# A fused audio-tower kernel: VectorE adds the embedding's bias on the way out of PSUM, gamma and beta move to the passes after it

## The reference

```python
# tokenizer: patches of 16 rows of x, stride 8, 124 tokens per batch element
y  = einsum('bpi,di->bpd', patches, W) + b                 # D = 256
h  = (y - mean(y)) * rsqrt(var(y) + EPS) * gamma + beta
# attention layer on the normalised h
n  = layernorm(h); q, k, v = n@Wq.T+bq, n@Wk.T+bk, n@Wv.T+bv
h  = h + softmax(q @ k.T / scale) @ v
# mixture of experts: 6 experts, the best 2 for each token
n  = layernorm(h)
p  = softmax(relu(n @ router_w1 + b1) @ router_w2 + b2); top_w, top_i = top_k(p, 2)
e  = relu(relu(n @ w1 + b1) @ w2 + b2) @ w3 + b3           # per expert
h  = h + sum(e[top_i] * softmax(top_w))
```

## Time and profile before

| what | value |
|---|---|
| three runs | 1249.2, 1250.46, 1252.42 us (median 1250.46) |
| profiled execution | 1249.82 us, of which the span from the first to the last instruction is 1248.0 us |
| PE busy | 1197.6 us, 96% of the span, 7792 instructions |
| DVE busy | 984.9 us, 79% |
| ACT busy | 893.4 us, 72% |
| POOL busy | 901.1 us, 72% |
| first half | up to about 600 us; PE idle 0.2 us between 300 and 480 us |

### The profile page before, as it was taken

The page is one execution under the profiler, slowest core; times in us unless marked ns, Lnnn a source line. Parts: engine busy times, 40 slices in busy tenths (PEclk is TensorE's granted clock), DMA queues, the critical chain, the costliest instruction groups (busy, mean ns, idle before and its releaser), DMA issues. The chain is left out here.

```text
span 1248.0 us, 27869 instructions
## 1 busy us (share of the span) xinstructions
PE 1197.6 (96%) x7792; PEld 1060.7 (85%) x7792; DVE 984.9 (79%) x3213; ACT 893.4 (72%) x2093; POOL 901.1 (72%) x684
## 2 busy tenths in 40 slices
PE   6999999999999999999789999999999999999993
PEld 5888988889888988887678888889888888888883
DVE  5678888888888988886796887778778777787773
ACT  4788888888888888887456667666676666766762
POOL 2227888888888888887788676767667667676776
PEclk9999999999999999999899999999999999999997
DMA  4334665554454545564589988776886797697655
GB/s 132 111 94 121 164 166 148 143 128 131 128 128 123 129 130 142 169 168 117 139 189 279 238 155 206 119 128 108 174 180 113 130 225 126 116 203 150 111 60 60
DMA packets 137190, 180.43 MB, mean 145 GB/s; under 512 B 38344, under 2 KB 103500, under 8 KB 137036
## 3 DMA queue, kind: packets, MB, share of 16 engines
q0 software_dynamic: 75456, 69.19, 34.5%
q1 hardware_dynamic: 60316, 108.67, 28.6%
q10 hardware_dynamic: 1264, 0.79, 0.2%
HBM read 159.01 MB, written 101.49 MB: 209 GB/s over the span
## 5 line engine op out<-in xcount | busy, mean ns | idle before, releaser
L570 POOL DMA_INDIRECT out<-yo,tail x268 | 432.5, 1614 | 169.1 <-issue 139.6
L522 POOL DMA_INDIRECT expert_rows<-rec,row_i x256 | 356.3, 1392 | 78.0 <-issue 67.2
L1003 ACT ACTIVATE h2v<-bank,small 128x512 f32<-128x512 f32 x134 | 92.3, 690 | 205.3 <-PE bank L793 189.8
L820 PE MATMUL bank<-w_sb,h_hi 128*128 128x256 f32 x1072 | 208.7, 288 | 3.5 <-issue 3.4
L793 PE MATMUL bank<-x_hi,w_sb 128*128 128x512 f32 x536 | 178.2, 394 | 6.1 <-DVE x_lo L1380 4.6
L793 PE MATMUL bank<-h_hi,w_sb 128*128 128x512 f32 x536 | 177.2, 391 | 1.8 <-issue 1.8
L820 PEld LDWEIGHTS bank<-w_sb,h_hi 128*128 128x128 f32 x1072 | 171.3, 191 | 4.4 <-issue 4.3
L820 PE MATMUL bank<-w_sb,h_lo 128*128 128x256 f32 x536 | 151.5, 283 | 0.0
L793 PEld LDWEIGHTS bank<-x_hi,w_sb 128*128 128x128 f32 x536 | 101.7, 190 | 27.9 <-issue 4.8
L793 PEld LDWEIGHTS bank<-h_hi,w_sb 128*128 128x128 f32 x536 | 100.9, 188 | 21.9 <-issue 1.9
L1009 ACT ACTIVATE yo<-yo,gcol 128x256 f32<-128x256 f32 x268 | 113.9, 498 | 4.5 <-DVE yo L1411 4.5
(11 more groups left out here) (193 smaller groups left out, 2975.9 us busy)
## 6 DMA issues: line engine op xcount, KB each, us to landing
w_sb<-split_weights SPq DMA_DIRECT2D x189, 512.0 KB
xg<-expert_rows SPq DMA_DIRECT2D x67, 530.0 KB
out<-h SPq DMA_DIRECT2D x32, 496.0 KB
split_weights<-half_w SPq DMA_DIRECT2D x36, 256.0 KB
small<-in_esmall SPq DMA_DIRECT2D x67, 134.0 KB
x_in<-in_x SPq DMA_DIRECT2D x32, 250.0 KB
expert_rows<-pad_rows SPq DMA_DIRECT2D x9, 530.0 KB
raw_w<-in_eweights SPq DMA_DIRECT2D x36, 128.0 KB
```

The costliest lines, as they stand in the source:

```text
L522: pool.indirect_dma_start(rows_dram, bass.IndirectOffsetOnAxis(ap=row_i[0:TOK, slot, j, k:k + 1], axis=0), rec[0:TOK, slot, j, :], None).t ...
L570: pool.indirect_dma_start(out, bass.IndirectOffsetOnAxis(ap=tail[:, t % TAILS, j, E8:].bitcast(I32), axis=0), yo[:, t % YO, j, :], None, c ...
L820: mm = pe.matmul(banks[6 + b][:, (j % 2) * D:(j % 2 + 1) * D], act[:, c, j * P:(j + 1) * P], w[:, 2, c, wh, :], start=(c == 0 and p == 0), ...
L1003: act.activation(h2v[:, m, :], banks[bank + m][:], ACT.Relu, bias=small[:, t % SLOTS, DC + m:DC + m + 1]).then_inc(S["h2_v"], 1)
```

## The change

The bias is loaded once into all 128 partitions (`bias_bc`) and centred there; the bias matmul and its operands go. VectorE's pass out of PSUM adds the bias instead of multiplying by gamma, and stands right behind the statistics of h instead of behind those of the attention. Gamma becomes the last factor of the h pass, and beta is added by two new instructions over h. ScalarE squares y out of SBUF, behind `pT` instead of ahead of `qT`. `shifts` (the column `nmr`) moves ahead of the split of x. `LN1_N` becomes 17.

```diff
-LN1_N, AV_N, TOPK_N, POS_N = 15, 14, 23, 4
+LN1_N, AV_N, TOPK_N, POS_N = 17, 14, 23, 4
...
-            sp.wait_ge(S["pool_const"], 1)
-            for r in (0, 32):
-                sp.dma_start(bias_raw["tok"][r:r + 1, :], tok_b).then_inc(S["tok_bias_loaded"], 16)
+            sp.dma_start(bias_bc[:], tok_b.to_broadcast([P, D])).then_inc(S["tok_bias_loaded"], 16)
...
                             for c in range(DC):
-                                product(into, [t[:, at + c:at + c + TOK] for t in (xT_hi, xT_lo)],
-                                        [proj["tok"][:, b, c, :] for b in range(2)], c == 0, False)
-                            if it == -1:
-                                pe.wait_ge(S["proj_low"], 2)
-                            mm = pe.matmul(into, ones_r[:, 0:TOK], bias_row["tok"][:], start=False, stop=True)
+                                mm = product(into, [t[:, at + c:at + c + TOK] for t in (xT_hi, xT_lo)],
+                                             [proj["tok"][:, b, c, :] for b in range(2)], c == 0, c == DC - 1)
...
-                if xa:
-                    g, slot, rnd = xa
-                    wait(act, S["rstd13"], deviations(g - 2))
-                    for j in range(GB):
-                        act.wait_ge(S["tok_ps"], g * 2 + j // 2 + 1)
-                        wait(act, S["squares"], g * GB + j)
-                        act.activation(square[0:TOK, :], banks[6 + j // 2][0:TOK, (j % 2) * D:(j % 2 + 1) * D], ACT.Square,
-                                       scale=D ** -0.5, accum_out=mv[0:TOK, 0, j, 1:2]).then_inc(S["squares"], 1)
                 if x1:
...
                     act.activation(pT[0:TOK + 1, :], banks[4][0:TOK + 1, 0:GT], ACT.Identity).then_inc(S["pT_sb"], 1)
+                if xa:
+                    g, slot, rnd = xa
+                    wait(act, S["rstd13"], deviations(g - 2))
+                    for j in range(GB):
+                        act.wait_ge(S["ln1"], g * LN1_N + 1 + j // 2)
+                        wait(act, S["squares"], g * GB + j)
+                        act.activation(square[0:TOK, :], y[0:TOK, j, :], ACT.Square,
+                                       scale=D ** -0.5, accum_out=mv[0:TOK, 0, j, 1:2]).then_inc(S["squares"], 1)
                 if x3:
...
+                    if it == 0:
+                        v.wait_ge(S["const_loaded"], N_CONST)
                     for j in range(GB):
                         v.wait_ge(S["ln1"], at + 1 + j // 2)
                         v.scalar_tensor_tensor(out=h[R, g % KEPT, j, :], in0=y[R, j, :], scalar=rstd[R, 0, j:j + 1],
-                                               in1=beta_bc[R, :], op0=ALU.mult, op1=ALU.add).then_inc(S["ln1"], 1)
+                                               in1=gamma_bc[R, :], op0=ALU.mult, op1=ALU.mult).then_inc(S["ln1"], 1)
+                    for pair in range(2):
+                        v.wait_ge(S["ln1"], at + 4 + 2 * pair)
+                        v.tensor_tensor(h[R, g % KEPT, 2 * pair:2 * pair + 2, :], h[R, g % KEPT, 2 * pair:2 * pair + 2, :],
+                                        beta_bc[R, :].unsqueeze(1).to_broadcast([TOK, 2, D]), ALU.add).then_inc(S["ln1"], 1)
...
                 if it == 0:
                     fold_weights()
                     shifts(0)
+                if xa:
+                    g, slot, rnd = xa
+                    for pair in range(2):
+                        v.wait_ge(S["tok_ps"], g * 2 + pair + 1)
+                        v.tensor_tensor(y[R, 2 * pair:2 * pair + 2, :],
+                                        banks[6 + pair][R, :].rearrange("p (b n) -> p b n", b=2),
+                                        bias_bc[R, :].unsqueeze(1).to_broadcast([TOK, 2, D]), ALU.add
+                                        ).then_inc(S["ln1"], 1)
                 if x4:
                     gates(*x4)
...
-
+                if x0 and it > 0:
+                    shifts(x0[0])
                 if xs:
...
-                if x0 and it > 0:
-                    shifts(x0[0])
                 if it == DRAIN - 2:
...
-                    for pair in range(2):
-                        v.wait_ge(S["squares"], g * GB + 2 * pair + 2)
-                        v.tensor_tensor(y[R, 2 * pair:2 * pair + 2, :],
-                                        banks[6 + pair][R, :].rearrange("p (b n) -> p b n", b=2),
-                                        gamma_bc[R, :].unsqueeze(1).to_broadcast([TOK, 2, D]), ALU.mult
-                                        ).then_inc(S["ln1"], 1)
```

More of the change, by code:

```diff
@@ L1049, in centre_bias, with statistics @@
                 v.wait_ge(S["tok_bias_loaded"], N_TOK_BIAS)
-                v.tensor_reduce(bias_mean[0:33, :], bias_raw["tok"][0:33, :], AX_X, ALU.add).then_inc(s, 1)
+                v.tensor_reduce(bias_mean[:], bias_bc[:], AX_X, ALU.add).then_inc(s, 1)
                 v.wait_ge(s, 3)
-                v.scalar_tensor_tensor(out=bias_raw["tok"][0:33, :], in0=bias_mean[0:33, :].to_broadcast([33, D]),
-                                       scalar=-1.0 / D, in1=bias_raw["tok"][0:33, :], op0=ALU.mult, op1=ALU.add
-                                       ).then_inc(s, 1)
+                v.scalar_tensor_tensor(out=bias_bc[:], in0=bias_mean[:].to_broadcast([P, D]), scalar=-1.0 / D,
+                                       in1=bias_bc[:], op0=ALU.mult, op1=ALU.add).then_inc(s, 1)
             centre()
             R = slice(0, TOK)
-            def statistics(which, src, s, at, g):
+            def statistics(which, src, s, at, made):
                 for j in range(GB):
-                    v.wait_ge(s, at - GB + 1 + j)
+                    v.wait_ge(s, at + made[j])
                     v.bn_stats(stats[R, which, j, :], src(j)).then_inc(s, 1)
@@ L1183, in step @@
                     centre_bias()
-                    low_bias("tok", 2)
-                    v.wait_ge(S["pool_const"], 22)
+                    v.wait_ge(S["pool_const"], 20)
+                    v.wait_ge(S["centred"], 4)
                 for n in chunks_of(it):
```

43 lines of the change are left out of this document (14 added, 29 removed).

## The result

The changed kernel takes **1346.7 us** (median of four runs, 1346.33 to 1347.13) against 1249.83 for the kernel before on the same chip. The ratio is 1.0775, with a 95% interval of 1.076 to 1.0791: 7.8% slower. The direction was as predicted; the time lies 58 us above the 1289 and 46 above the upper end of the range. The profiled execution has a span of 1344.6 us against 1248.0.

The account below looks back on a forecast made before the run. TensorE was taken to bound the kernel now; after the change, a ring through three engines. 27 periods of 18.94 us gave +35.9, the start made it +38.4, from 1249.8 to 1289 us; range 1281 to 1301.

Parts of the forecast that it names:

- The wrong count and its ring: ScalarE's last two squares wait on `ln1` until `nmr`, delaying `rhT` and TensorE's router layer 2: period 18.94 us.
- steps 1 to 8: Pieces of one period, from router layer 2 through `negmax`, beta, y, `nmr`, squares and `rhT` to TensorE's restart: 18.94 us.
- The likeliest case: Steady loop: 27 periods of 18.94 us, TensorE waiting 1.86 us for `rhT` in each; 1289 us in all, chance 0.72.
- The rival that the clock falls: TensorE's new wait lowers its clock: 1370 us if in every iteration, 1305 if in one of five; chance 0.07.
- the sum: 27 x 18.94 = 511.4 us against 475.5, +35.9; with the start +38.4, giving 1289 us.
- The rival's own size: Each fall of TensorE's clock, staying low for 3 us of work, costs 3 us more; 81 in all.
- TensorE's saving: Four bias matmuls fewer in each iteration: 0.48 us each time, 13 us in all if TensorE stays the bound.
- The start: Iteration 0: a y and four squares come ahead of xn1, less the matmuls saved: +2.5 us, bounds 0 to 5.
- All iterations alike: The first half's loop was taken as 27 equal periods of 18.94 us.
- GpSimd in the way: Beta passes lengthen GpSimd's scatters, so rstd and `nmr` slip: up to 0.5 us an iteration, 1302 us; chance 0.12.
- The count does not bite: Squares start with the first y: period 17.54 us, whole 1252 us, no change; chance 0.05.
- TensorE stays the bound: The saved matmuls come through in the loop: period 17.08 us, 13 us less, about 1240 us; chance 0.04.

Follow-up runs that it names:

- the count right: The changed kernel with the waits on `ln1` corrected, so the squares wait for their own y and xn1 for `nmr`: 1263.1 us, ratio 1.01.
- the eight matmuls: The changed kernel with eight unread matmuls of 128x512 on TensorE ahead of its wait for `rhT`: 1314.5 us, ratio 1.0512.
- the squares out of the way: The changed kernel with corrected `ln1` waits and ScalarE's four squares moved behind `rhT` and the half_w copy, ahead of xn1: 1246.47 us, ratio 0.9981.
- `rhT` held back: The kernel before with eight unread ScalarE squares of a constant ahead of `rhT` in each group: 1314.79 us, ratio 1.0523.
- four matmuls of 128x512: The changed kernel with four unread matmuls on TensorE ahead of its wait for `rhT`: 1342.25 us, ratio 1.0743.
- the short beta passes: The changed kernel with its two beta passes cut to 2 of 256 columns, `ln1` waits unchanged: 1294.65 us, ratio 1.0354.

## Why the prediction failed

- **The wrong count and its ring** (steps 1 to 8, 18.94 us). Right, place and size. Putting the count right takes 84 us away; the single pieces agree within 0.1 us; the ring at full clock is 20.54 - 1.5 = 19.0, and with most of the beta passes off it and the clock up it is 18.15.
- **The likeliest case had the clock up. This is the step that failed.** The rival that the clock falls was given 0.07, and it is what happened, behind 27 of 28 waits, at 1.5 us a period: 39 us that the sum put at nothing. The wait of 1.86 us that the sum gave was 1.90; its consequence was judged by one window, in which TensorE was busy 0.62 of 2 us and the clock stayed, against 22 to 24 us where it did not the earlier trace rows. Both were single places, and the first says nothing of what came just before and after. The runs show that without the eight matmuls every wait of 1.14 us or more at this place brought the clock down, and that already 0.93 us can do it; the two longest waits that did not, 2.09 and 2.01 us, stood behind eight dense matmuls. With the wait filled the clock stays at 1.00 and 32 us come back.
- **The rival's own size.** It had 3 us for each fall, from 3 us of work at half speed. It is 1.4 to 1.5: the clock is low for some 3.4 us of time, not for 3 us of full-speed work. With that, its time would have been 1289 + 26 x 1.5 = 1328, and the rest of the way to 1346.7 are the start, the long iterations and 0.1 us a period of the ring.
- **TensorE's saving.** 13 us were set for the matmuls if TensorE stayed the bound; with them gone alone the kernel gains 6 (0.9953), and with the squares out of the way the loop gains 7.
- **The start, +2.5 (0 to 5).** It was 9.1, outside its own bounds. The forecast mechanism is there: xn1 of iteration 0 starts at 30.07 instead of 25.58, behind squares that wait for y behind the folded weights, as these rows show. But it gives 4.5 in the first iteration, where 2.9 less 0.5 were set, and the next two add as much; TensorE is not full there, and at 30 to 35 and 45 to 50 us its clock is near 0.50. In the run with the count right it is 6.2, with the squares out of the way 2.1. How the rest divides between the chain and the clock is not shown.

```profile
26.16 1.28 DVE L1137 TENSOR_TENSOR y<-bank,tok_bias_bc 124x512 f32<-124x512 f32 x2
...
26.93 0.42 ACT L929 ACTIVATE square<-y 124x256 f32<-124x256 f32 x1 [4.31 <-DVE y L1137]
```

- **All iterations alike.** The sum took 27 equal periods. Five are 0.8 to 2.8 us longer than the rest, together 9 us, the longest of them (23.32) where the first scatters fall. That a ring has no slack to take up a late GpSimd or VectorE would explain it; it is argued, not shown.
- **GpSimd in the way (0.12).** In the kernel after it costs nothing: the scatter that begins inside a beta pass lasts 1.42 us, 0.1 more than the shortest and not 0.4, and the scatter beside `nmr` ends just as `nmr` does. With the clock kept up it cost 0.45 us a period, through the cast.
- **The count does not bite (0.05).** Its ring was put at 17.54; with the count put right it is 17.60, and the start and some longer iterations make the whole 1263 and not 1252.
- **TensorE stays the bound (0.04).** It needed `rhT` not to stand behind the squares; with that done and the count right, 1246.5 against its 1240. With `rhT` alone moved ahead it was 1276.3.

Not settled: why the same wait of 1.01 us lets the clock fall in one iteration and not in another, and why waits of 2 us behind eight matmuls did not. That it is so is shown, what decides it is not. Nor were the longer iterations taken apart.

## What to carry to other kernels

When a change brings a wait of about 1 us or more onto a TensorE that was full, price the clock with it: look for the granted clock behind several waits of that length in the trace, not one. The price of a fall is the work done in the low stretch at half speed (here 1.5 us of 3.4), every time the wait comes round, less what a later wait of the same engine takes up (0.7 of the 1.5 in the kernel before with `rhT` held back). Count the increments of a semaphore in the order in which the engine now issues them before trusting a `wait_ge` in moved code, and then look at what stands behind the waiting instruction: the same wrong count cost 84 us ahead of `rhT` and 2 to 4 us two instructions later. Work that depends on a longer chain goes behind whatever another engine is waiting for.

## What the runs showed of the hardware

- TensorE's clock fell to its lower level behind all 27 waits of 1.84 us and more in the kernel after. Shorter waits went both ways: 0.93 to 1.07 us behind four matmuls of 128x512 brought it down 21 times and left it up twice; 1.01 us in the kernel before 16 times and 11 times; with the short beta passes 0.97 to 1.21 us 10 times and 3 times, and 0.87 to 0.94 left it up all 12 times. Waits of 0.5 us, in the run with the count right, never brought it down. And once in each of the two runs with eight matmuls ahead of it, a wait of 2.09 us (476.07) and one of 2.01 us (464.97) left the clock at 1.00. A fall lasted some 3.4 us and cost TensorE 1.4 to 1.5 us of work; the period grew by as much where the ring through TensorE had no slack, and by 0.5 where it had.
- More work for TensorE made the kernel faster: eight matmuls a period in an idle stretch took 32 us off it, while four took 4.
- VectorE's cast of 124x8 float to int32 took 0.17 us outside a scatter or begun at most 0.25 us into one, and stood until the scatter's end when it began later: 0.74 us when begun 0.65 into it, 0.32 when begun 1.09 into it (the kernel after); the reciprocal and `nmr` behind it waited with it, while `nmr` ahead of it ran in 0.16 under the same scatter. The kernel before has the same twice, once as a cast of 0.52 us from 421.70 under a scatter that ends at 422.25. The Trainium skill, SBUF — State Buffer, section "Who interferes with whom", says that casts may take the port pair that VectorE shares with GpSimd, and that who comes second is blocked for the whole instruction; the late casts fit that; `nmr`, with its inputs both in SBUF, ran on under the same scatter.
- A ScalarE square of 124x256 lasts 0.42 us from SBUF and 0.38 from PSUM, and the next follows after 0.60 instead of 0.57: 0.03 more each, where 0.02 had been taken.
